# Bilinear corners summed by one VectorE operation in the patch rows and the tail of a four-layer block kernel

## The reference

```python
off = jnp.einsum('nchw,oc->nohw', inputs, w_grid) + b_grid      # where each of 9 taps reads
# px, py: the place of each tap in pixels
x0, y0 = floor(px), floor(py);  wx1, wy1 = px - x0, py - y0;  wx0, wy0 = 1 - wx1, 1 - wy1
sampled = (tap(x0, y0, wx0 * wy0) + tap(x1, y0, wx1 * wy0)
           + tap(x0, y1, wx0 * wy1) + tap(x1, y1, wx1 * wy1))   # 4 corners, weighted
out = conv(sampled, w_conv, stride 3)                           # 9 taps x 32 channels -> 32
x = x + out
```

## Time and profile before

| | |
|---|---|
| Median of 3 runs | 1876.15 us (1868.05 to 1881.27) |
| Profiled execution | 1873.85 us, span of its instructions 1872.0 us |
| PE busy | 1613.2 us, 86% of the span |
| DVE busy | 1459.5 us, 78% |
| POOL busy | 1201.2 us, 64% |
| ACT busy | 1107.2 us, 59% |
| Chain that ended last | PE 49%, DVE 13%, DMA 10% |
| Granted TensorE clock, mean | 0.948 of full |

### The profile page before, as it was taken

The page is one execution under the profiler, slowest core; times in us unless marked ns, Lnnn a source line. Parts: engine busy times, 40 slices in busy tenths (PEclk is TensorE's granted clock), DMA queues, the critical chain, the costliest instruction groups (busy, mean ns, idle before and its releaser), DMA issues.

```text
span 1872.0 us, 42695 instructions
## 1 busy us (share of the span) xinstructions
PE 1613.2 (86%) x15890; PEld 1326.5 (71%) x15890; DVE 1459.5 (78%) x3011; ACT 1107.2 (59%) x1547; POOL 1201.2 (64%) x1403
## 2 busy tenths in 40 slices
PE   4685488889898989889898998889889898988998
PEld 3544476688567976679666895578756896668998
DVE  5476378987898887987898778987879767987776
ACT  2011456576555865567655766557655676558886
POOL 2042366785677765785767766776667856777664
PEclk9787689999999998999999999999999999999999
DMA  6546855698656974689656976679655894235542
GB/s 138 124 113 158 206 174 157 173 225 200 190 164 187 247 220 137 175 214 223 192 154 177 254 201 167 176 185 250 190 148 164 213 221 144 80 87 167 147 144 83
DMA packets 284245, 326.14 MB, mean 174 GB/s; under 512 B 209444, under 2 KB 223780, under 8 KB 280192
## 3 DMA queue, kind: packets, MB, share of 16 engines
q1 hardware_dynamic: 240712, 228.88, 45.7%
q0 software_dynamic: 35856, 80.87, 17.2%
q10 hardware_dynamic: 7472, 13.67, 2.4%
HBM read 253.50 MB, written 56.40 MB: 166 GB/s over the span
## 4 chain that ended last, share of the span: by engine, by line
PE 49%; DVE 13%; DMA 10%; DVEq 7%; SPq 6%; POOL 6%; issue 6%; ACT 3%; ACTq 1%; POOLq 0%
PE bank L1344 27%; DMA words<-in_codebook,code 5%; PE bank L1472 5%; PE bank L1331 4%; DVE code L1215 3%; PE bank L1426 3%; DVEq L1214 3%; PE bank L1455 3%; PE bank L1328 3%; POOL fetched L631 3%; DVEq L1009 3%; SPq L453 2%; POOL words L654 2%; DMA y_patches<-yc 2%; PE bank L1315 2%
## 5 line engine op out<-in xcount | busy, mean ns | idle before, releaser
L631 POOL DMA_INDIRECT fetched<-row_pairs,corner x768 | 739.7, 963 | 419.8 <-DVE weighted L1004 217.5
L1344 PEld LDWEIGHTS bank<-lent,tent 128*128 128x128 f32 x6144 | 872.4, 195 | 95.2 <-issue 70.0
L1344 PE MATMUL bank<-lent,tent 128*128 128x160 f32 x6144 | 937.2, 308 | 2.5 <-issue 1.7
L763 ACT ACTIVATE tent<-lent,row_at_sb 128x768 f32<-128x768 f32 x512 | 448.6, 923 | 52.7 <-PE bank L1344 45.9
L996 DVE TENSOR_TENSOR strip<-bank,near 128x480 f32<-128x480 f32 x512 | 332.5, 651 | 124.9 <-PE bank L1344 120.9
L767 ACT ACTIVATE tent<-tent 128x1536 f32<-128x1536 f32 x256 | 380.0, 1484 | 20.6
L654 POOL DMA_INDIRECT words<-in_codebook,code x256 | 244.9, 957 | 112.5 <-DVE code L1215 63.2
L1010 DVE TENSOR_REDUCE samp<-strip 128x96 f32<-128x480 f32 x414 | 270.4, 653 | 39.2 <-issue 1.8
L1472 PE MATMUL bank<-cb,xs 64*128 64x512 f32 x512 | 221.4, 677 | 27.3 <-DVE code L1215 14.0
L842 ACT COPY xs<-xn 32x128 f32<-32x128 f32 x256 | 75.6, 295 | 235.7 <-PE bank L1472 218.0
L752 ACT COPY samp_t<-bank 96x384 f32<-96x384 f32 x256 | 120.1, 469 | 148.9 <-PE bank L1331 125.0
(11 more groups left out here) (149 smaller groups left out, 1241.3 us busy)
## 6 DMA issues: line engine op xcount, KB each, us to landing
lent<-z_rows SPq DMA_DIRECT2D x256, 384.0 KB
picked_weights<-arena SPq DMA_DIRECT2D x14, 1800.0 KB
arena<-picked_weights SPq DMA_DIRECT2D x21, 720.0 KB
arena<-windows SPq DMA_DIRECT2D x276, 50.0 KB, 2.0
arena<-xp SPq DMA_DIRECT2D x96, 136.0 KB
fetched<-row_pairs,corner POOLq DMA_INDIRECT x768
arena<-row_pairs SPq DMA_DIRECT2D x64, 160.0 KB
slice<-picked_weights SPq DMA_DIRECT2D x14, 720.0 KB
```

What stands on the lines that cost most here:

```text
L631: pool.indirect_dma_start(fetched[:, N % FETCHES, k].rearrange("p q c -> p (q c)"), None, pairs_dram[b % 2], bass.IndirectOffsetOnAxis(ap= ...
L763: act.activation(w[:, piece], zs[:, N % SPREADS, :], ACT.Abs, bias=row_at[:, piece:piece + 1])
L1344: m = pe.matmul(STRIPS[j % 3][:, XW * C * e:XW * C * (e + 1)], tent[:, N % TENTS, c, DENSE * d + e], picture[:, b % 2, i, c], start=(c == ...
```

## The change

`samp` gets a third piece of 96 numbers. For the tiles of the patch rows `row0` to `row3` and for those of the tail (`corners_added`), VectorE sums the four corners of `weighted` into that piece with one `tensor_reduce` ahead of the second half's column sum, behind a drain of its own; TensorE then transposes that piece once in place of the four transposes that add. Those are 10 tiles in each of groups 2 to 7, 3 in group 1 and the 39 of the tail: 102 of 256. All other tiles are as before. The new operation reads `weighted` as (tap, channel) outside and corner inside, so that two numbers read one after the other lie 96 x 4 = 384 bytes apart.

```diff
-        samp = sb("samp", [128, TURNED, HALVES * PARTK])
+        samp = sb("samp", [128, TURNED, (HALVES + 1) * PARTK])
...
+        def corners_added(N):
+            J = HALVES * N
+            if J >= LEFT:
+                return True
+            reached = (J + SHIFT) % (HALVES * GROUP_TILES) - SHIFT
+            return PLACE["row0"][0] <= reached and reached + 1 < PLACE["row3"][1]
+
...
+                if d == 1 and corners_added(N):
+                    dve.drain()
+                    dve.tensor_reduce(samp[:, N % TURNED, HALVES * PARTK:],
+                                      weighted[:, N % TURNED].rearrange("p q k c -> p (k c) q"), AX.X, ALU.add)
                 if not added_by_pool(J):
                     if N >= TURNED:
                         dve.wait_ge(samp_turned, N - TURNED + 1)
...
+                if corners_added(N):
+                    pe.transpose(PT[0:PARTK, 256:384], samp[:, N % TURNED, HALVES * PARTK:], ident[:]
+                                 ).then_inc(samp_turned, 1)
+                    return
                 for q in range(CORNERS):
                     m = pe.matmul(PT[0:PARTK, 256:384], weighted[:, N % TURNED, q].rearrange("p k c -> p (k c)"), ident[:],
                                   start=(q == 0), stop=(q == CORNERS - 1), is_transpose=True)
```

## The result

The changed kernel takes 1864.92 us (median of 22 runs, 1847.19 to 1881.88) against 1876.28 us before (22 runs, 1857.98 to 1881.82). The ratio is 0.9943, with a 95% interval of 0.9924 to 0.9963: about 11 us, or 0.6%, faster, inside the 1% that the text ahead calls no change. 1865 was said. Ratios here leave out executions over 1.5% above a kernel's lowest, which are six of the changed kernel (1876.77 to 1881.88 us) and none of the 22 before; by the means of all 22 each (1867.1 and 1874.5 us) the gain is 7 us, ratio 0.996.

The account below looks back on a forecast made before the run. TensorE was taken as the bound, holding half the chain, with VectorE the tail's new bound. Tail -2 and patch rows -9 make -11 us: 1863 from the profiled 1873.85, said as 1865 for the median; range 1846 to 1888.

Parts of the forecast that it names:

- The removed transposes: In 102 tiles TensorE drops three transposes of 0.109 us, 0.33 us a tile, 33.3 us at most.
- The price of the sum: VectorE's new sum takes 875 ns, between 553 and 955; with its drain 0.96 us a tile.
- The tail: Last 39 tiles: VectorE becomes the bound at 4.04 us a tile against TensorE's 4.15 before; -2 us in all.
- The last step: End of the tail: last tile's samples come 0.96 us later and are turned 0.33 faster, +0.6 us.
- The patch rows: Pairs of rows -6 us, group 1 -1, less VectorE waiting in `y` -2: together -9 us.
- What a pair gains or loses is then 6.1 less its idle time, but never better than -1.6: Per pair of patch rows: VectorE gets 4.8 us, 1.3 of its idle time is unusable; TensorE loses 1.6.
- first pairs: First two patch rows of groups 2 to 7: VectorE has little idle time, together +0.7 us.
- second pairs: Last two patch rows of groups 2 to 7: VectorE has more idle time, together -6.9 us.
- What would show it: Signs: sum's mean 875 ns; tail chain moves to VectorE, four tiles in 16.2 us; TensorE's waits for L996 new.
- A: Rival: the sum costs 0.55 us, as if the jumps were free; nearly all 33.3 us arrive, 1843 us; chance 0.15.
- B: Rival: the wide jump costs more, 1.3 us a sum; +26 us, 1902 us; chance 0.15.
- C: Rival: TensorE, VectorE and ScalarE lock, each waiting a little for the next; no change, about 1876 us; chance 0.15.

Follow-up runs that it names:

- e4: Changed kernel without VectorE's new sum, TensorE still turning only one corner (output not the reference's): ratio to before 0.9863.
- e3: Changed kernel with the new sum reading the same count of numbers side by side, without the jump (output not the reference's): ratio to before 0.982.
- e2: Changed kernel with the change only in the 63 tiles of the patch rows, the tail as before: ratio to before 0.9949.
- e5: Changed kernel keeping VectorE's new sum, but TensorE again turns all four corners: ratio to before 1.0045.
- e11: Changed kernel with the sum, in the patch rows, only in row2 and row3 (5 tiles a group), and in the tail: ratio to before 0.9962.
- e1: Changed kernel with the change only in the 39 tiles of the tail, the patch rows as before: ratio to before 1.0004.
- e9: Changed kernel with the sum made by two adds of numbers side by side, without a drain of its own: 1850.39 us, ratio to before 0.9878.
- e6: Changed kernel with VectorE making the new sum twice, the second into an unused piece: 1922.55 us, ratio to before 1.0256.
- e12: Changed kernel with the same sum moved behind the first half's column sum, without its own drain: ratio to before 0.9897.

## Why the prediction was right, and where it was not

**The removed transposes** were 0.33 us a tile where TensorE is the bound: e4's 20 tiles take 76.4 us against 83.0, 0.33 each. Right.

**The price of the sum** was taken as 875 ns out of 553 to 955 and was 840, 1.79 ns a number behind the fixed 153; from start to start 0.93 in place of 0.96. Right, and e3 shows how much hung on the choice between the ends: 0.982 at the low one. Of the two pages of the Trainium skill weighed against each other, "VectorE: DVE Perf Modes", section "Mode 1× (REGULAR) — the baseline", fits e3's 553 ns and not the 840 of a jump of 384 bytes; "SBUF — State Buffer", section "Door 1: The DMA port swizzle (why `[64,N]` ≈ `[32,N]`)", names such a cost, and the two numbers bear it out. No run here varies the width of the jump, so the 16 bytes are not shown.

**The tail** was to be VectorE's at 4.04 us a tile and was at 4.00, and TensorE's lead swallowed the convolutions: in 20 tiles VectorE waits for nobody but for one gap of 0.4 us that no engine is named for. From the first multiply to the end the change is -2.4 (4.0 won, 1.6 lost) where -2 was said. The last step was mis-sized, +1.6 for +0.6: behind the last sums TensorE stands for 3.42 us, and its transposes and products then go at the lower clock (TensorE's timeline at the end, after; in brackets the idle time and what ended it):

```profile
1845.79 0.66 PE L1339 MATMUL bank<-ident_sb,samp 128*96 128x128 f32 x2 [3.42 <-DVE samp L1021]
...
1847.23 1.51 PE L1326 MATMUL bank<-samp_t,wc 96*32 96x128 f32 x24 [0.56 <-ACT samp_t L759]
```

The same 24 products took 0.86 us before. The granted clock from 1843.5 on is 0.50, that is 1.2 GHz, and was 0.96 over the same end before.

**The patch rows** were right in the sum (-8 said for the pairs and `y`, -5.5 in one profile, -1.3 in e2's, -5 to -14 by e2's interval) by two errors that cancel. The step that failed in size is "What a pair gains or loses is then 6.1 less its idle time, but never better than -1.6". It takes all of VectorE's waits for TensorE in a pair as room. In the first pairs they are not: over the six, VectorE's waits for TensorE were 29.6 us and are 17.6 after the change. So 12.0 us of the 27.9 that VectorE got (30 sums of 0.93) found room, and the other 15.9 are nearly all of the +16.3. Group 3 had 3.2 us of them, and after the change still has 2.4:

```profile
DVE strip L1003 <- PE bank L1359: 1.4, 3, 0.6
DVE yc L1130 <- PE bank L1441: 1.0, 2, 0.5
```

TensorE for its part stands at one place, around `normalise`, for VectorE's column sum: 1.9 us in group 3, where it stood 1.0 before (with no engine named), and over the six first pairs 12.0 us where it was 9.5. Both engines wait, in turn, within one pair, and what is waited at one place does not make room at another. And there is a cost that no term of the prediction had: the clock behind that wait. TensorE's timeline in the first pair of group 3, and the busy times of the stretch behind its wait:

```profile
613.47 0.40 PE L1339 MATMUL bank<-ident_sb,samp 128*96 128x128 f32 x2 [1.92 <-DVE samp L1021]
614.14 5.10 PE L1359 MATMUL bank<-lent,tent 128*128 128x160 f32 x24
621.62 3.53 PE L1359 MATMUL bank<-lent,tent 128*128 128x160 f32 x24
```

```profile
615.10:617.10 2.00, 2.00 (x9) 2.00 (x8) 1.54 (x6) 1.92 (x4) 1.70 (x2) 0.50 1.11 337
```

The granted clock fell to 0.50 (1.2 GHz), and 24 products took 5.10 us in place of 3.5. Before, the first pairs had a mean clock of 1.00 in five groups of six and 0.94 in one, whose 30.5 us were the longest; after, 0.95 in all five that normalise. In e2 and e5, with the same sum, it is 0.95 in five of ten such pairs. Over these three kernels the pairs with the fall are 32.2 us long on average and those without 31.3, so some 4 us of the +16.3 (0.9 in four groups more than before) are the clock, as an estimate. It is in part chance: before, it fell behind a wait of 1.9 us in group 5 and not behind one of 2.3 in group 4. So the first pairs paid 2.7 us a group and not 0.1. And the floor of -1.6 was wrong for the second pairs: TensorE leaves the first ones ahead, VectorE runs from 637.1 to 659.1 without a recorded wait (4.2 us for TensorE in the same rows before; over the six, some 40 us before and 3 after), and the second pairs gave back 3.0 us each. e11 takes the lead away and finds 5.3 us in place of 17.9. For group 1, -1 was said: from its first gate to the residual it takes 62.4 us after and 62.5 in e2, where it takes 65.0 before and 64.5 in e1. That two wrong terms add up to nearly the right sum is luck.

**What would show it.** The mean of the sum and the 4.00 us a tile did (from one convolution's products, at 1785.31, to the next, at 1801.31, are 16.0 us for four tiles, where 16.2 was said). One sign was badly chosen: that the chain would go over to VectorE and TensorE show waits. The chain in the tail, after:

```profile
1781.55 0.11 PE bank L1342
1781.66 3.65 PE bank L1359 x24
1785.31 0.79 PE bank L1326 x24
...
1786.57 3.26 PE bank L1359 x24
```

It still names TensorE. Some groups of 24 products take 0.3 to 0.4 us more than others (3.65 for 3.26); that these are stalls for VectorE, not recorded as idle, is inferred from the 4.00 us a tile against the 3.82 of e4. TensorE's busy time says nothing either, 80.82 of 80.90 us; its weight loads do, 74.92 of 80.9 us where e9 has 74.41 of 76.4. The engine that bounds was seen by VectorE's gapless timeline.

**The rivals.** A fell by the measured price, and e3 shows that its time (1843 said, 1845.46 measured) was right for its condition. B fell likewise, and e6 shows the other side. C is contradicted by e12, e4 and e9, where the tail keeps to the slower engine's own pace within 0.03 us a tile.

## What to carry to other kernels

Moving work from the bounding engine to its neighbour is worth the gap between the two, and then the neighbour's price decides: read it from an operation with the same access, not the same count, since here a jump between numbers made 553 ns into 840 and took more than half of what could be had (e4 has 26 us, the changed kernel 11). In the tail, two passes over numbers that lie side by side (362 and 259 ns), placed where a drain stands already, beat one with a jump and a drain, 76.4 us against 80.9 for 20 tiles. And room is not the sum of an engine's waits: where two engines waited for each other in turn, less than half of the waits (12.0 of 29.6 us) could be used.

## What had not been expected of the hardware

The times of one kernel spread over 20 to 35 us, and the traces show one place where it comes from. From the residual behind the second layer's convolution (L1190) to the first score maximum (L1213) a group mostly takes some 14 to 15 or some 17 us (12.5 to 18.0 over all kernels here), before and after, in changing groups: 3 of 7 groups are near 17 in the profile before, 1 in that of the changed kernel, 5 in e2's. A quick and a slow group of the changed kernel, 2 and 3, by stretch:

```profile
480.00:483.70 3.70, 3.70 (x33) 2.02 (x36) 2.89 (x8) 2.15 (x3) 2.64 (x3) 1.00 0.68 232
692.80:696.50 3.70, 3.70 (x14) 3.63 (x15) 1.32 (x5) 1.79 (x2) 1.70 (x2) 0.50 0.50 175
```

and TensorE's 12 products of one half in each:

```profile
479.05 1.90 PE L1359 MATMUL bank<-lent,tent 128*128 128x160 f32 x12
```

```profile
692.73 3.57 PE L1359 MATMUL bank<-lent,tent 128*128 128x160 f32 x12
```

In both groups TensorE had stood for the rows of the second layer, 3.0 us in group 3 and 3.5 in group 2. In group 3 its clock was then 0.50 (1.2 GHz); in group 2 it was 1.00 there and fell later. The stretch adds up to 102.4 us over groups 1 to 7 in the profile of the changed kernel, the least of all kernels here, to 107.9 before, and to 113.7 at most (e5 and e11). These up to 11 us do not follow the change. The two profiles alone would have told 20 us for it; the 22 executions of each told 11 or, by the means, 7.
